# The turns around the chunk inverse on VectorE, and a new merge of the streams

## What is computed

```
def step(state, inp):
    q_t, k_t, v_t, g_t, b_t = inp
    state = state * jnp.exp(g_t)[..., None, None]
    v_err = (v_t - jnp.einsum('bhkv,bhk->bhv', state, k_t)) * b_t[..., None]
    state = state + jnp.einsum('bhk,bhv->bhkv', k_t, v_err)
    o_t = jnp.einsum('bhkv,bhk->bhv', state, q_t) * scale
    return (state, o_t)
...
normed_reads = _rmsnorm(reads, mnorm_scale).reshape(b, s, d)
fused = jnp.concatenate([normed_reads, normed_p20], axis=-1)
projected = fused @ out_W + out_b
return jax.nn.sigmoid(gate_in) * projected
```

## Time and profile before

| | us |
|---|---|
| median of 3 runs | 5939.71 (5938.71, 5939.71, 5969.02) |
| the profiled execution's own time | 5967.04 |
| its span | 5965.4 |
| TensorE busy | 5158.8 |
| VectorE busy | 2928.0 |
| ScalarE busy | 1756.1 |

### The profile page before, as it was taken

The page is one execution under the profiler, slowest core; times in us unless marked ns, Lnnn a source line. Parts: engine busy times, 40 slices in busy tenths (PEclk is TensorE's granted clock), DMA queues, the critical chain, the costliest instruction groups (busy, mean ns, idle before and its releaser), DMA issues. The chain is left out here.

```text
span 5965.4 us, 218898 instructions
## 1 busy us (share of the span) xinstructions
PE 5158.8 (86%) x98967; PEld 3328.7 (56%) x98967; DVE 2928.0 (49%) x6701; ACT 1756.1 (29%) x2887; POOL 538.5 (9%) x657
## 2 busy tenths in 40 slices
PE   5999999999999999999999658999999999999400
PEld 3555565656656565656565535666666666666300
DVE  6667676767667676767676384000000001000255
ACT  3333333333333343434333101212212211211122
POOL 0000000000000000000000001111111111111376
PEclk9899899999999999999998679999999999999755
DMA  1000000000000000000000001111111111111365
GB/s 30 18 15 22 19 18 22 19 22 15 22 19 20 21 18 22 18 22 19 22 19 18 14 4 40 50 33 50 49 35 47 36 49 50 35 50 35 96 190 174
DMA packets 170008, 220.32 MB, mean 37 GB/s; under 512 B 32306, under 2 KB 148083, under 8 KB 169075
## 3 DMA queue, kind: packets, MB, share of 16 engines
q1 hardware_dynamic: 122994, 106.02, 5.6%
q0 software_dynamic: 29312, 84.97, 4.9%
q10 hardware_dynamic: 16896, 16.78, 0.8%
HBM read 138.50 MB, written 67.11 MB: 34 GB/s over the span
## 5 line engine op out<-in xcount | busy, mean ns | idle before, releaser
L1407 PE MATMUL bank<-gathered_T,w1s 128*128 128x512 f32 x2048 | 928.8, 613 | 67.6 <-DVE gathered_T L1350 67.6
L1418 PE MATMUL bank<-w2s,hidden_T 128*128 128x256 f32 x4096 | 894.6, 379 | 0.0
L1418 PEld LDWEIGHTS bank<-w2s,hidden_T 128*128 128x128 f32 x4096 | 775.7, 190 | 117.8 <-issue 15.3
L1377 ACT ACTIVATE hidden_T<-bank,b_expert 128x512 f32<-128x512 f32 x512 | 352.0, 687 | 1544.4 <-PE bank L1407 1544.4
L1407 PEld LDWEIGHTS bank<-gathered_T,w1s 128*128 128x128 f32 x2048 | 399.3, 196 | 559.5 <-issue 557.8
L1357 DVE TENSOR_TENSOR result_rows<-bank,b2s 128x512 f32<-128x512 f32 x128 | 88.6, 692 | 1217.7 <-PE bank L1418 1217.7
L900 PE MATMUL bank<-xT_and_z_out,ctrlW 128*128 128x512 f32 x768 | 383.9, 623 | 4.3 <-issue 4.3
L900 PE MATMUL bank<-np,p20W 128*128 128x512 f32 x768 | 375.3, 619 | 7.1 <-DVE conv_out L693 4.4
L1350 DVE COPY gathered_T<-bank 128x512 f32<-128x512 f32 x128 | 88.6, 692 | 557.8 <-PE bank L1396 541.9
L1136 POOL MEMSET tri<- 128x128 f32 x1 | 0.2, 209 | 3430.5 <-POOLq L337 3430.5
L1038 PEld LDWEIGHTS bank<-yb,bd_v 32*32 32x32 f32 x16384 | 188.7, 114 | 210.5 <-issue 209.9
(11 more groups left out here) (287 smaller groups left out, 7624.7 us busy)
## 6 DMA issues: line engine op xcount, KB each, us to landing
expert_rows<-result_rows SPq DMA_DIRECT2D x64, 512.0 KB, 2.9
x<-L_attn_hidden SPq DMA_DIRECT2D x33, 512.0 KB, 3.8
out_squares<-L_attn_hidden SPq DMA_DIRECT2D x32, 512.0 KB, 3.6
x_rows<-x SPq DMA_DIRECT2D x32, 512.0 KB, 3.1
x_rows_sb<-x_rows SPq DMA_DIRECT2D x32, 512.0 KB, 4.3
out<-out_rows ACTq DMA_DIRECT2D x32, 512.0 KB, 3.1
w1s<-L_ffn_w POOLq DMA_DIRECT2D x8, 1024.0 KB, 5.9
w2s<-L_ffn_w POOLq DMA_DIRECT2D x8, 1024.0 KB, 7.8
```

The source lines that it names most:

```text
L1377: nc.scalar.activation(hT[:, j, m, :], ring["h", j, m][:, :], ACT.Gelu, bias=b1e[:, par, m:m + 1]).then_inc(hT_ready, 1)
L1407: ins = nc.tensor.matmul(ps[:, :], w1s[:, par, k, m * P:(m + 1) * P], xgT[:, j, k, :], start=k == 0, stop=k == 1)
L1418: ins = nc.tensor.matmul(ps[:, i * D:(i + 1) * D], hT[:, j, m, s0:s0 + P], w2s[:, par, m, :], start=m == 0, stop=m == MT - 1)
```

## The change

Both turns around the inverse are taken from TensorE and made by VectorE's `transpose`, which turns each 32x32 block in itself. For that the key product is written by one more VectorE instruction: L797 is split in two, one into a new tile `a_rows` (A by position and group, the groups innermost), one into `apk`, which shrinks from 48 to 32 columns a group. VectorE transposes `a_rows` into the new tile `turned` in two instructions of 128x512, ScalarE copies it negated into `fx`, the elimination runs on a matrix laid out by columns, and two more transposes of 128x512 bring the inverse back into `turned`, from which ScalarE fills `bd`. Four new signals (`a_turned`, `x_ready`, `t_turned`, `bdt_ready`) take the place of the bank counts. Ring B loses four of its 24 entries, and gets one for padding that VectorE frees. The identity products L989 and L999 are gone. All four strings in `ORDERS` are new.

```
@@ -192,9 +192,11 @@
         FX = sb("fx", P, W2)
-        apk = sb("apk", P, G, 3 * CHUNK)
+        a_rows = sb("a_rows", P, CHUNK, G)
+        apk = sb("apk", P, G, TILE)
         bdkb = sb("bd_kb", P, G, TILE)
         tmp = sb("inverse_tmp", P, 4 * 56)
+        turned = sb("turned", P, W2)
         YB = sb("yb", P, G, TILE)
@@ -221,7 +223,7 @@
         g16 = lambda t: t[:, 0:G * CHUNK].rearrange("p (g i) -> p g i", i=CHUNK)
-        X = FX[:, :].rearrange("p (h i c) -> p h i c", i=CHUNK, h=HPT // 2)
+        X = FX[:, :].rearrange("p (c b i) -> p b c i", i=CHUNK, b=4)
         F, EGv = g16(FX), g16(EG)
@@ -268,9 +271,9 @@
 
-        def ring(r, order, at):
+        def ring(r, order, at, pads_by="act"):
             while len(order) % len(at):
-                order.append((("pad", len(order)), "act"))
+                order.append((("pad", len(order)), pads_by))
             return Bank(order, at, filled[r], {w: emptied[r, w] for w in ("act", "dve")})
@@ -281,19 +284,18 @@
         order += [(("mm1", t), "dve") for t in range(8)]
-        order += [(("aT", t), "act") for t in range(2)] + [(("T", t), "act") for t in range(2)]
         order += [(("Y", t), "act") for t in range(4)] + [(("M", t), "dve") for t in range(4)]
-        rb = ring("B", order, banks[3:6])
+        rb = ring("B", order, banks[3:6], "dve")
         order = [(("L", c), "act") for c in range(NCH)] + [(("on",), "act")]
...
         ORDERS = dict(
-            pe=("CACBACCBBCCBABBABCABBABCABBACBBCCCACCACC" "ABBCACCCBBCBBACBBCBBAABBACBBAABCBAABCBAA"),
-            dve=("CBCAAACCABBABAAAABBABCBBAABCBBBBBCBBBBCB" "BBBCAABCBCCAAAAACABAAAACACACACBABBAAABBA" "AA"),
-            act=("BBACBBBBBCCAAAAAAAAABBCBABCCACCCCBBBAABB" "BACCAAACC"),
-            sp="AACC")
+            pe=("CACBCCABCCBBBBABBABBABBACCACCACCCCACCACA" "CCCCCBBCBABBABABBABBAABBACCBBAABCABA"),
+            dve=("CBCACACBBAABABABABBBACBBACBBBACBBBBCBBBC" "ABBBCBBCCBBBAAAAAAAAACAAAAACBAAACCBCAABB" "AABBAA"),
+            act=("BACBABBBBBACCAABAABACAAACBCBCACCCBBBAABB" "AACBAACCC"),
+            sp="CAAC")
 
@@ -525,11 +527,10 @@
 
-                    act.wait_ge(b_dve, rb.done(u, ("mm1", 7)))
                     for t in range(2):
-                        act.wait_ge(rb.filled, rb.full(u, ("aT", t)))
-                        A(X[:, :, 8 * t:8 * t + 8, :].rearrange("p h i c -> p i h c"), rb["aT", t][:, :].rearrange("p (i h c) -> p i h c", i=8, c=CHUNK),
-                          ACT.Copy, scale=-1.0).then_inc(b_act, 1)
+                        act.wait_ge(a_turned.sem, a_turned.of(u, t + 1))
+                        A(X[:, :, :, 8 * t:8 * t + 8], half(turned, t).rearrange("p (i b c) -> p b c i", b=4, c=CHUNK), ACT.Copy,
+                          scale=-1.0).then_inc(x_ready.sem, 1)
                         yield
@@ -540,10 +541,10 @@
                     for t in range(2):
-                        act.wait_ge(rb.filled, rb.full(u, ("T", t)))
-                        ps = rb["T", t][:, :].rearrange("p (c g) -> p g c", g=G)
+                        act.wait_ge(t_turned.sem, t_turned.of(u, t + 1))
+                        ps = half(turned, t).rearrange("p (c g) -> p g c", g=G)
                         A(bdT[:, 0, :, 8 * t:8 * t + 8], ps, ACT.Copy, scale=pmask[:, 0:1])
-                        A(bdT[:, 1, :, 8 * t:8 * t + 8], ps, ACT.Copy, scale=pmask[:, 1:2]).then_inc(b_act, 1)
+                        A(bdT[:, 1, :, 8 * t:8 * t + 8], ps, ACT.Copy, scale=pmask[:, 1:2]).then_inc(bdt_ready.sem, 1)
                         yield
@@ -794,26 +795,35 @@
                         gs = slice(8 * t, 8 * t + 8)
-                        V.tensor_tensor(apk[:, gs, 0:TILE].rearrange("p g (a i) -> p g a i", a=2), ps[:, :, 0:TILE].rearrange("p g (a i) -> p g a i", a=2),
-                                        F[:, gs, :].unsqueeze(2).broadcast_to([P, 8, 2, CHUNK]), ALU.mult)
-                        V.tensor_tensor(apk[:, gs, TILE:], ps[:, :, TILE:], F[:, gs, CHUNK - 1:CHUNK].broadcast_to([P, 8, CHUNK]), ALU.mult)
+                        V.tensor_tensor(a_rows[:, :, gs].rearrange("p i g -> p g i"), ps[:, :, 0:CHUNK], F[:, gs, :], ALU.mult)
+                        V.tensor_tensor(apk[:, gs, 0:CHUNK], ps[:, :, CHUNK:TILE], F[:, gs, :], ALU.mult)
+                        V.tensor_tensor(apk[:, gs, CHUNK:], ps[:, :, TILE:], F[:, gs, CHUNK - 1:CHUNK].broadcast_to([P, 8, CHUNK]), ALU.mult)
                         V.tensor_tensor(bdkb[:, gs, :].rearrange("p g (a i) -> p g a i", a=2), ps[:, :, TILE:].unsqueeze(2).broadcast_to([P, 8, 2, CHUNK]),
...
 
-                    dve.wait_ge(b_act, rb.done(u, ("aT", 1)))
+                    dve.wait_ge(b_dve, rb.done(u, ("mm1", 7)))
+                    dve.wait_ge(bdt_ready.sem, bdt_ready.before(u))
+                    for t in range(2):
+                        V.transpose(half(turned, t), a_rows[:, 8 * t:8 * t + 8, :].rearrange("p i g -> p (i g)")).then_inc(a_turned.sem, 1)
+                        yield
+                    dve.wait_ge(x_ready.sem, x_ready.of(u))
                     dve.sem_inc(passed, 1)
-                    for h in range(HPT // 2):
-                        V.memset(FX[:, h * CHUNK * CHUNK:(h + 1) * CHUNK * CHUNK:CHUNK + 1], 1.0)
+                    for b in range(4):
+                        V.memset(FX[:, b * CHUNK:(CHUNK - 1) * (4 * CHUNK + 1) + b * CHUNK + 1:4 * CHUNK + 1], 1.0)
 
...
                         n = CHUNK - 1 - j
-                        t = tmp[:, 0:n * (HPT // 2) * j].rearrange("p (h i c) -> p h i c", i=n, h=HPT // 2)
-                        sb_.then(V.tensor_tensor(t, X[:, :, j + 1:, j:j + 1].broadcast_to([P, HPT // 2, n, j]),
-                                                 X[:, :, j:j + 1, 0:j].broadcast_to([P, HPT // 2, n, j]), ALU.mult))
-                        sb_.then(V.tensor_tensor(X[:, :, j + 1:, 0:j], X[:, :, j + 1:, 0:j], t, ALU.add))
+                        t = tmp[:, 0:4 * n * j].rearrange("p (b c i) -> p b c i", b=4, c=j)
+                        sb_.then(V.tensor_tensor(t, X[:, :, j:j + 1, j + 1:].broadcast_to([P, 4, j, n]),
+                                                 X[:, :, 0:j, j:j + 1].broadcast_to([P, 4, j, n]), ALU.mult))
+                        sb_.then(V.tensor_tensor(X[:, :, 0:j, j + 1:], X[:, :, 0:j, j + 1:], t, ALU.add))
                         if j == CHUNK - 2:
                             dve.sem_inc(inv_ready.sem, 1)
+                        yield
+                    dve.wait_ge(inv_ready.sem, inv_ready.of(u))
+                    for t in range(2):
+                        V.transpose(half(turned, t), half(FX, t)).then_inc(t_turned.sem, 1)
                         yield
@@ -833,7 +843,7 @@
                         gs = slice(16 * t, 16 * t + 16)
-                        V.tensor_tensor(MQ[:, gs, :], MQ[:, gs, :], rb["M", t][:, :].rearrange("p (g n) -> p g n", n=TILE), ALU.add).then_inc(b_dve, 1)
+                        V.tensor_tensor(MQ[:, gs, :], MQ[:, gs, :], rb["M", t][:, :].rearrange("p (g n) -> p g n", n=TILE), ALU.add).then_inc(b_dve, 1 + (rb.pads if t == 3 else 0))
                         if t == 3:
@@ -979,36 +987,14 @@
 
-                    pe.wait_ge(b_dve, rb.done(u, ("mm1", 7)))
-                    pe.sem_inc(passed, 1)
-                    for t in range(2):
-                        ps = rb.take(pe, u, ("aT", t))
-                        pe.sem_inc(passed, 1)
-                        for j in range(8):
-                            for r in HALVES:
-                                ins = T.matmul(ps[r, j * G:(j + 1) * G], apk[r, :, 8 * t + j], ident[r, r], start=True, stop=True)
-                        ins.then_inc(rb.filled, 1)
-                        yield
-
-                    pe.wait_ge(inv_ready.sem, inv_ready.of(u))
-                    for t in range(2):
-                        ps = rb.take(pe, u, ("T", t))
-                        pe.sem_inc(passed, 1)
-                        for j in range(8):
-                            for r in HALVES:
-                                ins = T.matmul(ps[r, j * G:(j + 1) * G], FX[r, 8 * t + j::CHUNK],
-                                               ident[r, r], start=True, stop=True)
-                        ins.then_inc(rb.filled, 1)
-                        yield
-
-                    pe.wait_ge(b_act, rb.done(u, ("T", 1)))
+                    pe.wait_ge(bdt_ready.sem, bdt_ready.of(u))
                     pe.sem_inc(passed, 1)
...
                             for r in PAIRS:
-                                ins = T.matmul(ps[r, j * TILE:(j + 1) * TILE], bd[r, 16 * t + j, :], apk[r, 16 * t + j, CHUNK:], start=True, stop=True)
+                                ins = T.matmul(ps[r, j * TILE:(j + 1) * TILE], bd[r, 16 * t + j, :], apk[r, 16 * t + j, :], start=True, stop=True)
                             if j == 7:
```

5 lines of the change are left out of this document (2 added, 3 removed).

## The result

The changed kernel is a little slower: 5996.65 us median (5974.96 to 6007.79, 8 runs) against 5944.39 (5921.61 to 5977.11, 8 runs) taken beside it, ratio 1.0083, interval 1.0059 to 1.0107, about 50 us. Forecast were 5810 and a range up to 5945. The profiled execution has a span of 6000.8 us.

A forecast was written before the change was run, and what follows sets the result against it. TensorE bounds, VectorE not far behind. A unit goes 102.7 - 7.9 + 3.5 = 98.3 us; 31 x 4.4 = 136, taken as 130, so 5940 - 130 = 5810 us. Range 5700 to 5945.

The forecast's parts named there:

- Stretch two keeps its content, and I leave it as it is: TensorE from the four output projections to the next key products: 54.6 and 56.8 us before, expected near 56.
- wrong if stretch two grows by more than 2 us: Stated failure sign for the part from output projections to next key products, which was expected near 56 us.
- Two other signs: Stated failure signs: a wait for `fx` before L813, or for `bd` before Y.
- Stretch one: TensorE from key products to output projections: from 46.9 us to 39, plus 3.5 for lost clock, near 42.
- VectorE's row: VectorE's instructions from first evacuation to last state step, summed as unbroken work: 32.2 us, ending 33.3 after the key products.
- The waits of TensorE "for the state": In the state steps before the projections: expected to grow from 0.83 us apiece to 2 or so.
- VectorE's order takes it back: Rival: in-order waits for `fx` and late `oT` copies cost 4 us a unit before the projections; 5930 us, 18%.
- 7.5 us a unit lie on the path: Identity products L989 and L999 on TensorE: removing them frees 233 us over 31 steps, if nothing else waits.
- stay, with SBUF in place of PSUM as source: ScalarE's six copies into `fx` and `bd`: no cost, covered by ScalarE being 40% busy.
- The strided write: VectorE writing `a_rows` with 256-byte spacing: put at nothing; rival 1.1 us a unit, 34 in all, 5844 us, 6%.
- The clock: State steps before the projections: granted clock about 0.8, costing 3.5 us a unit.
- The slower rival: Clock stays low through the projections: 6.8 us lost before them, 4.5 more in them; 6045 us, 13%.

The follow-up runs named there:

- the kernel with the pair together: Changed kernel with one TensorE letter moved, so the third spreading product comes directly before the fourth: 5913.76 us, ratio 0.9993 to the kernel before.
- the run under the old merge: The changed kernel's turns on VectorE with the engine orders of the kernel before, only the needed letters altered: 5945.34 us, ratio 1.0036 to the kernel before.
- both runs of the pair: Third and fourth spreading products put together in the changed kernel (5913.76 us, ratio 0.9993), and parted in the kernel before (6000.33 us, ratio 1.013).

## Why the prediction was wrong

**The step that failed** is the sentence "Stretch two keeps its content, and I leave it as it is". Its content was kept and its adjacency was not. With the pair put together stretch two fell by 3.0 us a unit (61.66 to 58.69), of which 2.2 are the spreading products. The other 2.1 stand in the kernel with the pair together as idle time before M (1.5 us a unit instead of 0.8) and before Y (0.5 instead of 0.1, of it 0.3 for `bd`), the products for the gate L1072 (2.8 instead of 2.3) and the projections (9.5 instead of 8.9), at a clock of .899 instead of .908. That they belong to the new merge, not to the turns, the run under the old merge bears out (57.01); which of its moves brings them was not separated. The prediction had named the test, "wrong if stretch two grows by more than 2 us"; it grew by 5.1. Two other signs came true as well: VectorE waited for `fx` before L813 (22.8 us in 25 units), and Y for `bd` (8.5). I had compared the orders for what comes in and goes out of each stretch, not for which products stand next to each other.

**Stretch one** came out at 42.4 us, as forecast (39 + 3.5), by luck, for the working was wrong. VectorE's row, 32.2 us by the sum, was busy 30.3 but took 34.9: the waits in it, put at nothing ("almost without a gap"), were 4.6 us, and with seven of the fourteen elimination steps left out it took as long. The waits of TensorE "for the state" that were to grow to 2 us show as 2.6 us in 25 units; what grew is the wait for ring C's banks, which ScalarE empties (28.5 us), and idle time with no releaser shown. The rival "VectorE's order takes it back" described this, with ScalarE copying `oT` late behind `fx`, and gave it 18%. It would have come out at 5930; with the split pair's 53 to 77 us on top that is 5983 to 6007, and 5997 were measured. The agreement is in part chance: the rival put its 4 us into stretch one, which kept to the forecast, while the 2.1 us beside the pair came in stretch two.

**"7.5 us a unit lie on the path"**: the products ran without idle time before them, which shows that they delay what follows, not that what follows could use the time. With 6.2 us of them removed and nothing added, they gave 3.1 to 3.3.

**ScalarE's six copies were to "stay, with SBUF in place of PSUM as source", at no cost**: each became 0.5 us dearer, 3.1 us a unit, worth some 0.5% of the time or less; and the two into `fx` did not stay as they were, their reads became strided. The cover, ScalarE at 40% busy, was the wrong measure: the copies stand ahead of the copies that free ring C's banks.

**The strided write** of `a_rows` costs 358 ns against 269 for the same size written densely, 0.7 us a unit where I had put nothing and the prediction's estimate by the rule of the Trainium skill gave 1.1. The rule of the Trainium skill (SBUF — State Buffer, section on the DMA port swizzle), that an access which crosses to a new 16-byte line pays a penalty, holds here, and the copies out of `turned` fit it too: strided reads or writes of SBUF at 1.08 to 1.21 us, dense ones at 0.62.

The row I judged by, L814 with 128x56 at a mean of 238 ns, mixes two things. In the first elimination step (j = 1) it writes single elements 64 bytes apart, in the last (j = 14) runs of fourteen; in the timeline of before:

```profile
1061.21 0.26 DVE L814 TENSOR_TENSOR fx<-fx,inverse_tmp 128x56 f32<-128x56 f32 x1
...
1073.25 0.22 DVE L814 TENSOR_TENSOR fx<-fx,inverse_tmp 128x56 f32<-128x56 f32 x1
```

Over the 32 units these two average 256 and 218 ns, 38 ns for 56 elements or 0.7 ns an element, and `a_rows` pays 89 for 128, 0.7 again. (L814 reads `fx` in the same pattern as it writes it, so this pair can't part reading from writing; the one into `a_rows` is the write alone.) A stride's price stood in the trace of before, and the mean of the group hid it; L812, taken as the dense one, is such a mean too, 249 and 218 ns. On VectorE it costs no time that shows in this kernel, since 5 us less there changed stretch one by nothing.

**The clock**: .927 over stretch one, with the norm sum (L910 with `z_in`, 88.0 us in 25 units) at 3.5 us, near its low-clock 3.78. The windows part clock and waits: of the 7.5 us taken from stretch one 4.0 were gained, 2.0 became idle time (4.65 to 6.68) and 1.5 went into longer products, 0.9 of it in the norm sum. I had put 3.5 on the clock and nothing on the waits; the two together came out at the forecast length. The slower rival (low clock through the projections) had the right sign and the wrong mechanism: the projections lost 0.4 us a unit, not 4.5.

**Transposes** (0.67 and 0.71 us) were right, and so were the evacuations apart from the strided write (0.27 us each).

## What to carry to other kernels

When a schedule is written anew, compare not only what each engine does in a stretch but which small products are neighbours: the pair with different quarters of the array's rows ran together here (1.13 us for both) only with nothing between them, and one letter, 0.9 to 1.3% of the time, decided between "no change" and "slower". Before counting a removed product as gain, ask what the chain around it does meanwhile; where waits and the clock share what is freed, as here, half was a fair guess; the test is to remove the work with nothing put in its place. And price an instruction whose pattern or source changes by a row with the same stride, taken by itself: the mean of a group can hide two patterns.

## What the runs showed of the hardware

- Two spreading products (32 rows by 128 columns, 512 elements) side by side take 1.13 us at full clock and 2.08 at the lower level; parted by a step of 32x32 products each takes as long by itself (1.12 and 2.07). The Trainium skill (TensorEngine Tiling (Array Packing), Key Properties) says that different tiles can run in parallel and that a change of the tiling mode drains the engine; both runs of the pair agree with the first, and none shows a drain apart from it.
- ScalarE's copy of 128x512 within SBUF takes 0.62 us densely and 1.08 to 1.21 with a stride on either side. Read with 256 bytes between elements it takes 1.2 out of SBUF and 0.67 out of PSUM (L546 after and before).
- VectorE's product written with 256 bytes between elements takes 358 ns for 128x128 against 269 in dense runs; read and written with 64 bytes between, 256 against 218 for 128x56 (L814 before): 0.7 ns an element in both.
- Some 6.2 us of dense products in the state steps cost stretch one 0.4 us and raised its granted clock from .922 to 1.000.
- VectorE's block transpose of 128x512 takes 0.67 to 0.71 us.
